# One of four token blocks of a selective scan: states weighted by C on GpSimd and summed by TensorE's transposes in PSUM, in place of VectorE's sums

## What is computed

```python
def step(h, inp):
    xt, dtt, Bt, Ct = inp
    dA = jnp.exp(dtt[:, :, None] * A[None])
    h = h * dA + (dtt * xt)[:, :, None] * Bt[:, None, :]
    y = jnp.einsum('bds,bs->bd', h, Ct)     # the sum over the 16 states
    return (h, y)
```

## Time and profile before

| what | value |
|---|---|
| median of 3 runs | 6002.64 us |
| the three runs | 6000.39, 6002.64, 6003.43 us |
| span of the profiled execution | 6003.3 us |
| VectorE busy | 5250.3 us (87%) |
| TensorE matmuls busy | 4882.5 us (81%) |
| GpSimd busy | 3613.3 us (60%) |
| ScalarE busy | 2899.3 us (48%) |

### The profile page before, as it was taken

How to read it: one execution, slowest core, us unless ns; L and a number is a source line. 1 busy time by engine, 2 the same in 40 slices (tenths; PEclk the granted TensorE clock), 3 DMA queues, 4 the chain that set the end, 5 groups by cost and what they waited for, 6 DMA issues and landing times.

```text
span 6003.3 us, 80311 instructions
## 1 busy us (share of the span) xinstructions
PE 4882.5 (81%) x21508; PEld 3165.1 (53%) x21508; DVE 5250.3 (87%) x6743; ACT 2899.3 (48%) x4931; POOL 3613.3 (60%) x2815
## 2 busy tenths in 40 slices
PE   2999999999987777777777777877777787787767
PEld 1788888888863444444444444444444444444444
DVE  9666666666654999999999999999999999999998
ACT  1111111111115666675666666666675666656654
POOL 5233333333323777777777767777777777767785
PEclk9999999999998899999999999999999999999978
DMA  2111111111111112111121211212111121211111
GB/s 61 41 41 42 42 42 42 42 42 42 42 54 63 54 55 73 53 53 57 60 66 54 70 52 59 65 57 70 53 53 57 59 66 54 70 51 61 55 60 50
DMA packets 192158, 327.26 MB, mean 55 GB/s; under 512 B 24032, under 2 KB 56800, under 8 KB 187632
## 3 DMA queue, kind: packets, MB, share of 16 engines
q1 hardware_dynamic: 191728, 322.51, 17.2%
HBM read 254.25 MB, written 68.19 MB: 54 GB/s over the span
## 4 chain that ended last, share of the span: by engine, by line
DVE 32%; issue 16%; PE 13%; POOL 4%; ACT 3%; DVEq 2%; DMA 1%; SPq 0%; ACTq 0%; POOLq 0%
DVE hs L1072 18%; DVE acc L1085 11%; PE ht L1192 5%; POOL v L883 3%; PE mm L1181 3%; PE mm L1133 2%; DVEq L763 2%; PE mm L1141 1%; ACT decay L1013 1%; DVE xc L1044 1%; DVE rtb L1061 1%; PE mm L1156 1%; PE mm L1149 1%; PE mm L1173 0%; POOL dt L896 0%
## 5 line engine op out<-in xcount | busy, mean ns | idle before, releaser
L883 POOL TENSOR_TENSOR v<-u,b_rep 128x512 f32<-128x512 f32 x2048 | 2563.1, 1273 | 916.2 <-DVE hs L1072 627.2
L1072 DVE TENSOR_TENSOR_SCAN hs<-decay,carry,v 128x512 f32<-128x512 f32 x2048 | 2599.8, 1270 | 78.1 <-POOL v L883 36.4
L1192 PEld LDWEIGHTS ht<-ident,hs 128*128 128x128 f32 x8192 | 1020.4, 149 | 1968.7 <-issue 1291.4
L1192 PE MATMUL ht<-ident,hs 128*128 128x128 f32 x8192 | 1363.4, 293 | 760.3 <-DVE hs L1072 528.5
L1013 ACT ACTIVATE decay<-dt,a_neg 128x512 f32<-128x512 f32 x2048 | 1387.6, 685 | 985.3 <-DVE hs L1072 972.5
L1085 DVE SCALAR_TENSOR_TENSOR acc<-ht,c_now,acc 128x512 f32<-128x512 f32 x2048 | 1480.6, 723 | 38.8 <-PE ht L1192 37.3
L469 ACT ACTIVATE sg<-gate 128x512 f32<-128x512 f32 (+1 forms) x192 | 108.0, 562 | 1331.8 <-PE up L515 1331.8
L1133 PE MATMUL mm<-x_in,w_in 128*128 128x512 f32 x1024 | 553.1, 638 | 92.4 <-DVE xc L1044 50.0
L1181 PE MATMUL mm<-w_out,yt 128*128 128x512 f32 x1024 | 553.6, 639 | 53.8 <-DVE xc L1044 35.1
L1149 PE MATMUL mm<-w_in,x_z 128*128 128x512 f32 x1024 | 539.8, 618 | 0.0
L105 POOL TENSOR_TENSOR h<-h,h_small 128x1408 f32<-128x1408 f32 x64 | 166.2, 2597 | 439.9 <-DVE h_small L99 439.9
(11 more groups left out here) (129 smaller groups left out, 6906.9 us busy)
## 6 DMA issues: line engine op xcount, KB each, us to landing
b_rep<-ssm_d SPq DMA_DIRECT2D x512, 256.0 KB, 3.8
rtb<-res_d SPq DMA_DIRECT2D x128, 256.0 KB, 3.0
xt<-in_L_attn_x SPq DMA_DIRECT2D x64, 256.0 KB, 2.8
xnt_d<-xntb SPq DMA_DIRECT2D x64, 256.0 KB, 2.7
rt<-in_L_attn_x SPq DMA_DIRECT2D x64, 256.0 KB, 2.6
res_d<-rt SPq DMA_DIRECT2D x64, 256.0 KB, 2.0
x_in<-xnt_d SPq DMA_DIRECT2D x16, 1024.0 KB, 4.8
x_z<-xnt_d SPq DMA_DIRECT2D x16, 1024.0 KB, 4.9
```

What stands on the lines that cost most here:

```text
L883: nc.gpsimd.tensor_tensor(v[k % 2][:, j, :], u[g][:, j, :], b_rep[k % 4][:, :], ALU.mult).then_inc(v_ready, 1)
L1072: nc.vector.tensor_tensor_scan(h[k % 2][:, j, :], decay[n % 4][:, :], v[k % 2][:, j, :], carry[:, s, GD * g + j:GD * g + j + 1], ALU.mult, ...
L1192: last = nc.tensor.transpose(ht[n % 2][:, j, :], h[k % 2][:, j, t * P:(t + 1) * P], ident[:, :])
```

## The change

For the last of the four token blocks (t = 3, `LT`) VectorE's multiply-add is gone from all slots but the last of each group. In its place GpSimd multiplies the states of that block by C in place (`weigh`, one instruction of 128x512), with C's row loaded by a new DMA `load_c` into `c_rep`, and TensorE's transposes of that block accumulate over the 16 slots of a group in a PSUM bank `y`. One `tensor_tensor` of VectorE adds `y` to `acc` after the 16th. The bank for `y` is taken from `ht`, which now has one bank in place of two. Where it stands in the queues: GpSimd runs `drive(k)` and then `weigh(k - 2)`, before the entries of `POOL_AT`.

```diff
-    ht = [psum(f"ht{p}", [P, GD, P]) for p in range(2)]
+    ht, y = psum("ht", [P, GD, P]), psum("y", [P, GD, P])
...
+        def load_c(c, k):
+
+            wait(sp, weighted, c.at(32, k - 3))
+            row = k % NS
+            sp.dma_start(c_rep[k % 4][:, :],
+                         ssm_rows(c, row, row + 1)[:, LT * P:].broadcast_to([P, P])).then_inc(c_loaded[k % 4], 16)
...
+                if k + 1 < SLOTS:
+                    if c.exists(NC):
+                        load_c(c, k + 1)
...
+        def weigh(c, k):
+
+            wait(pool, c_loaded[k % 4], c.at(128, 16 * (k // 4) + 16))
+            wait(pool, carried, c.at(32, k + 1))
+            wait(pool, scanned, c.at(128, 4 * k + 4))
+            block_ = h[k % 2][:, :, LT * P:]
+            nc.gpsimd.tensor_tensor(block_, block_, c_rep[k % 4][:, :].unsqueeze(1).broadcast_to([P, GD, P]),
+                                    ALU.mult).then_inc(weighted, 1)
...
+                done, m = (c, k - 2) if k >= 2 else (c.plus(-1), k + SLOTS - 2)
+                if done.exists(NC):
+                    weigh(done, m)
...
-            else:
-                wait(dve, summed, c.at(128, n - 3))
-            wait(dve, turned, c.at(128, n + 1))
-            nc.vector.scalar_tensor_tensor(out=acc[g][:, t, :], in0=ht[n % 2][:, :, :].rearrange("p j d -> p (j d)"),
-                                           scalar=c_now[:, t, s:s + 1], in1=acc[g][:, t, :],
-                                           op0=ALU.mult, op1=ALU.add).then_inc(summed, 1)
+            elif t < LT:
+                wait(dve, summed, sums(c, g, s - 1, t))
+            if t < LT:
+                wait(dve, turned, c.at(128, n + 1))
+                nc.vector.scalar_tensor_tensor(out=acc[g][:, t, :], in0=ht[:, :, :].rearrange("p j d -> p (j d)"),
+                                               scalar=c_now[:, t, s:s + 1], in1=acc[g][:, t, :],
+                                               op0=ALU.mult, op1=ALU.add).then_inc(summed, 1)
+            elif s == NS - 1:
+                wait(dve, turned, c.at(128, n + 1))
+                nc.vector.tensor_tensor(acc[g][:, t, :], y[:, :, :].rearrange("p j d -> p (j d)"), acc[g][:, t, :],
+                                        ALU.add).then_inc(summed, 1)
...
-            wait(pe, scanned, c.at(128, 4 * k + 4))
-            wait(pe, summed, c.at(128, n - 1))
-            for j in range(GD):
-                last = nc.tensor.transpose(ht[n % 2][:, j, :], h[k % 2][:, j, t * P:(t + 1) * P], ident[:, :])
+            g, s = k // NS, k % NS
+            if t < LT:
+                wait(pe, scanned, c.at(128, 4 * k + 4))
+                if t:
+                    wait(pe, summed, sums(c, g, s, t - 1))
+                else:
+                    wait(pe, summed, sums(c, g, s - 1, LT - 1) if s else c.at(2 * GROUP_SUMS, GROUP_SUMS * g - 1))
+                for j in range(GD):
+                    last = nc.tensor.transpose(ht[:, j, :], h[k % 2][:, j, t * P:(t + 1) * P], ident[:, :])
+            else:
+                wait(pe, weighted, c.at(32, k + 1))
+                if s == 0:
+                    wait(pe, summed, c.at(2 * GROUP_SUMS, GROUP_SUMS * g))
+                for j in range(GD):
+                    last = nc.tensor.matmul(y[:, j, :], h[k % 2][:, j, t * P:(t + 1) * P], ident[:, :], is_transpose=True,
+                                            start=(s == 0 and j == 0), stop=(s == NS - 1 and j == GD - 1))
```

More of the change, by code:

```diff
@@ L659, in phase_b @@
     b_rep = [sb(f"b_rep{p}", [P, CL]) for p in range(4)]
+    c_rep = [sb(f"c_rep{p}", [P, P]) for p in range(4)]
     dt_rep = sb("dt_rep", [P, CL])
@@ L685, in phase_b, with sums @@
     b_loaded = [sem(f"b_loaded{p}") for p in range(4)]
-    v_ready, decay_ready, scanned, turned, summed, carried = (
-        sem(s) for s in ("v_ready", "decay_ready", "scanned", "turned", "summed", "carried"))
+    c_loaded = [sem(f"c_loaded{p}") for p in range(4)]
+    v_ready, decay_ready, scanned, weighted, turned, summed, carried = (
+        sem(s) for s in ("v_ready", "decay_ready", "scanned", "weighted", "turned", "summed", "carried"))
+    LT = NT - 1
+    GROUP_SUMS = NS * LT + 1
+    def sums(c, g, s, t):
+        return c.at(2 * GROUP_SUMS, GROUP_SUMS * g + (LT * s + t + 1 if t < LT else GROUP_SUMS))
     MM = [(0, "ip", 0), (4, "ip", 1), (7, "cv", 0), (10, "yt", 1, 0), (11, "ip", 2), (14, "cv", 1), (17, "yt", 1, 1),
@@ L860, in part @@
                     load_b(c.plus(1), k + 3 - SLOTS)
+                if k + 1 < SLOTS:
+                    if c.exists(NC):
+                        load_c(c, k + 1)
+                elif c.plus(1).exists(NC):
+                    load_c(c.plus(1), 0)
         over_chunks(sp, part)
@@ L890, in extra @@
                 wait(pool, z_ready, o.at(4, 2 * g + j // 2 + 1))
-                wait(pool, summed, o.at(128, 64 * g + 61 + j))
+                wait(pool, summed, sums(o, g, NS - 1, j))
                 nc.gpsimd.tensor_tensor(sz[:, j, :], acc[g][:, j, :], sz[:, j, :], ALU.mult).then_inc(y2_ready, 1)
@@ L1096, in part @@
                 if n == 3 and c.exists(NC):
-                    wait(dve, summed, c.at(128, 0))
+                    wait(dve, summed, c.at(2 * GROUP_SUMS, 0))
                     wait(dve, ct_copied, c.at(1, 1))
```

## The result

The changed kernel takes **6287.4 us** (median; 6279.2 to 6297.1) against 6002.0 us before: ratio **1.0478** (95%: 1.0463 to 1.0493), 285 us slower. The forecast was 6110 (5925 to 6215). The side was right, the size was not, and the time lies above the range. The profiled execution has a span of 6277.5 us, 274.2 more than before.

The account below looks back on a forecast made before the run. VectorE was taken to set the scan phase's time, with GpSimd running ahead. 6003 - 307 (sums removed) + 12 x 26.0 + 4 x 23.0 (waits in chunks) + 10 (halo) = 6110 us; range 5925 to 6215.

Parts of the forecast that it names:

- B's share: Slots 9, 10, 12, 14: B's loads arrive late behind stores, so VectorE waits 11.4 us a chunk, 182 in all.
- The first scan behind the branch: Slot 0 of a loop turn: VectorE's own gap of 3.7 us plus 1.3 of waiting for the weigh chain.
- What costs little: Part of the prediction on small costs: one bank of ht, loads of C, and halo, for which 10 us was added.
- L: Time from the end of weigh to the scan waiting for it, through block 3's transposes and hand-over: 0.85 us.
- the sums' waits at the branch: Block 0's sum after the loop's branch waits 6.7 us for TensorE, in each of twelve turns.
- the scans' waits: Waits of slots' first scans for weigh and block 3's transposes, in slots 9 to 14, 24, 29 to 0, 2, 3, 7.
- halo and copy: VectorE's short convolution instructions, held up more often because GpSimd is busier: 10 us added for halo.
- a worse case: 128 halos each held up by 0.4 us more: 50 us, named but not counted.
- The gap of 6.8 us: TensorE's gap after its last instruction of a loop turn, taken to start later because that instruction waits for weigh.
- Rival (a): TensorE's gap at the branch ends with VectorE's and isn't moved: 80 us fall away, 6030 us; chance 0.15.
- one bank of `ht` at nothing: TensorE's transposes wait for the sum before; 0.13 + 0.65 + 0.04 fits in the scan of 1.19, so no cost.
- Rival (c): Everything tighter than counted: weigh at 1.6 and TensorE at half clock after long waits, 6190 to 6240 us; chance 0.14.

Follow-up runs that it names:

- e3: Changed kernel with the loads of B and C issued ahead of the residual's stores and loads in SyncE's queue: 6100.1 us, ratio 1.0168.
- e9: Changed kernel with TensorE's products put ahead of block 3's transposes in every fourth position, where that block is turned: 6245.6 us, ratio 1.0395.
- e2: Kernel before with a fifth GpSimd multiplication in each slot, whose result nobody uses: 6145.9 us, ratio 1.0246.
- e4: Changed kernel with VectorE's halo and its copy written as scalar_tensor_tensor with a PSUM operand: 6266.3 us, ratio 1.0452.
- e17: Changed kernel with weigh's own tile, later block 3 transposes, loads before stores, VectorE's short instructions with a PSUM operand, and a prefetch hint at the branch: 5805.7 us.
- e1: Kernel before with one bank of ht in place of two, all sums still on VectorE: 6066.4 us, ratio 1.0116.
- e16: Changed kernel with weigh's own tile, later block 3 transposes, loads before stores, and halo, copies and keep with a PSUM operand; no hint: 5798.7 us.

## Why the prediction missed

**Right.** Weigh's price (1.23 forecast, 1.27 measured with its overlap). The mechanism: a lead of GpSimd of nearly two slots cut to less than one, so that idle time that had been free is VectorE's. The slots, mostly: waits stand at 9 to 12, 14, 24, 30, 31, 0, 2, 3 and 7, and B's share of them is right in size (182 forecast; 187 by e3, a third of it at sums that the term didn't have). The first scan behind the branch: 3.7 + 1.3 = 5.0 forecast, 5.4 measured. GpSimd at 67% (forecast near 70).

**The step that failed first** is in "What costs little": "Each miss at half clock is about 0.5; I count none", and with it L, which ends at the first scan of the slot and has no product in it. Behind a late block 3, TensorE comes out of its idle time at half clock (1.12 for 0.65, so 1.2 GHz for 2.4), does the products of that position, and only then block 0. Outside the branch the forecast had no wait of a sum at all; the runs show 169 us there, in most slots with a late weigh. e9 shows that it is the products: with them moved, 156 us of the sums' waits are gone, and also that this order of the queue isn't free, since the scans get 117. How much is the half clock and how much the order was not run apart; in slot 9 it is about 1.8 and 0.9 of 2.7 us, by the estimate above.

That the waits were only 61 us short is partly luck, since two terms were too large: the sums' waits at the branch (80 forecast, 34 added) and the scans' waits (324 forecast, 261 added).

**The second** is halo and copy: 75 us for 10. The prediction had the mechanism and even a price of a worse case (50), but took the hold-up as rare and as one GpSimd instruction long. e2 shows that one more GpSimd instruction a slot is enough for more, and the traces that a hold-up lasts until GpSimd stands idle. Taken out alone it is worth 21 us (e4), so it is a part of the balance and not a cause of its own.

**The third** is the branch, and it erred to the other side. The gap of 6.8 us was taken as a constant that moves with TensorE's last instruction. It did move, but shrank to 3.4 on average, so that the waits behind the branch grew by 4.8 us a turn and not by 8.0, 39 us less in all. Why it shrank, no run tells; e17 shows that with the chain repaired the gap has no measurable cost. Rival (a), the gap isn't moved, was wrong too, since the gap does follow block 3's late transposes.

**The fourth**, one bank of `ht` at nothing, cost 66 us where it could be measured alone (e1), at the branch and in small gaps and not in the sums' waits that the prediction checked. How much of the last 41 us of the balance is this one, no run tells.

Rival (c), "everything is tighter" (6190 to 6240), was the nearest in mechanism (the half clock; the scans started 1.0 to 1.46 us after weigh for an L of 0.85), with the wrong reason for the other half (weigh did not take 1.6).

## What to carry to other kernels

When work moves to an engine that has free time but whose result others then wait for, add up the chain from its last input to the *last* user in each queue behind it, not to the first: here the scan was late by 3.85 us and the sum behind it by 2.03 more. Before giving such a change up, take the chain apart (a tile of its own, the consumer a position later, loads ahead of stores): the same change went from 4.8% slower to 3.4% faster, and to 1.8% faster than the kernel before with the same cures. Waits that a producer's lead hid are worth almost nothing before (14 us) and a lot after (187), so price each cure in the kernel in which it will stand, and give the kernel before the same cures before crediting the change.

## What the runs showed of the hardware that was not expected

A copy of 128x64 on VectorE took 5873 ns on average and up to 11057 in e2 beside an uninterrupted stream of GpSimd multiplications of 1273 ns, and ended only when that stream paused; it took 195 ns as a `scalar_tensor_tensor` with an operand in PSUM (e16). A halo of 3 columns took up to 4744 ns in the changed kernel. TensorE's gap behind the branch was 6.8 us in the kernel before, 3.4 in the changed one (41.1 / 12) and 5.0 in e16 (60.1 / 12), and a prefetch hint removed its row in all three kernels that had it there. One bank less for the transposes cost the kernel before 1.2% (e1) with next to no more waiting of the sums for them (42.0 us for 38.8).
